# Routing four graphs at a time, and a second bank for the values product, in a graph-attention and mixture-of-experts kernel

## The chip, the cores and the metric

The kernel runs on one core of one Trainium2 chip. The metric is the device time of one execution in microseconds (us). The engines are called by their short names: PE (matrix products), DVE (vector), ACT (scalar, activations), POOL (GpSimd) and SP (the queue that issues most transfers).

## The reference, cut to what matters

```python
# x: 64 graphs x 128 nodes x 512, adj: 64 x 128 x 128, 16 heads of 32
h = layernorm(x)
a = q(h) @ k(h).T * 512**-0.5 + (adj + adj)      # per head, 128 x 128
a = softmax(where(any(a != 0), a, -inf))
x = x + (a @ v(h)) @ Wo.T
h = layernorm(x)                                  # 8192 tokens
s = maximum(h @ gate_W + gate_b, 1e-4)            # 8 experts
p = softmax(s); top 2 experts of each token
w = maximum(p, 0.1); w = w / (sum of w over the two)
out = x + sum over the two of w * (h @ expert_W[e] + expert_b[e]) / 2
```

## The kernel before, in words

The program has two phases. Phase A does the attention of the 64 graphs and the routing of their tokens; phase B does the experts' products over the token lists that phase A wrote to memory (`x_lists`). The change touches phase A alone.

**Turns and quarters.** Every engine's program in phase A is one loop, `for t in range(-6, 72)` over turns and `for c in range(4)` over the quarters of a turn. In turn t the scores and exponentials belong to graph t, the transposes of the probabilities to graph t-1, the products with values (`times_v`, into bank `ps_o`) and the copy `oT` to graph t-2, the output projection, residual and second norm to graphs t-3 and t-2. The projections go by pairs of graphs, one unit of 24 matmuls in each quarter (`big`): in an even turn Q, Q, V, V, in an odd turn O, K, O, K. Two banks `ps_p` take them in alternation: a unit waits until the unit two quarters earlier has been read (`wait_bank`). In the first and third quarter of the odd turn stand the two O units; quarter 1 and 3 of an even turn also transpose the normalised rows (`transposes`, "X", into `ps_m`). A unit of K or Q is read by ACT (high part) and then by DVE (`low_part`, the low part), one quarter after it was made, and on DVE behind that quarter's `attention_max`.

**The two halves of V.** A V unit makes 256 columns in a `ps_p` bank and then 264 columns (256 values and 8 gate columns), called `G_V`, in `ps_g`. Both V units of a pair use the same `G_V`, so the second half of V unit 1 waits for `v_done` of V unit 0, that is for ACT's three copies of it (L654 to L659). ACT makes them in the next quarter, behind the exponentials of the quarter before, and those wait for DVE's `amax`.

**Routing.** DVE routes the tokens of a pair p of graphs in five functions of small instructions (128 x 16 elements, mostly), each of which waits for the one before it: `gate_scores(p)` in quarter 2 and `choose(p)` in quarter 3 of the odd turn 2p+5, then `weigh(p)` and `find_places(p)` together in quarter 1 of the even turn 2p+6, all of them last in their quarter. Between them ACT takes one exponential (`eexp`), and PE counts the tokens per expert in quarter 1 of turn 2p+6 with three small matmuls into `G_P`, 24 columns of `ps_g` (L595 to L597), once `choose` has written `mask_sum`. V unit 0 of that turn waits, ahead of its second half, for the first step of `find_places`, because `G_P` shares a bank with `G_V`. `find_places` adds the running fill of each expert's list and writes the rows `pos`. POOL then issues the scatters, `scatter(p, a)`: two indirect DMAs a graph from `xn2`, one graph in each turn, in turn b+6 for graph b. `xn2` has 4 buffers, `pos` has 2, `gate_x` has 8.

**Ahead of the loop's steady part**, PE turns Wo, multiplies it with the gate's weights (`wo_times_gate`, with the columns `O_W` and `O_S` in `ps_o`), and `times_v` of graph 0 waits until these are read. **At the end of phase A**, from turn 62 on, DVE also splits the experts' weights (`expert_lo`, L974), in the order of `LO_AT`, and then makes the table of tiles for phase B (L1046 to L1069) and the last two splits.

Of the kernel before, what the change touches and what calls it, by code (L numbers as in the profile page):

```python
# [17 lines left out]
P = 128  # L18
B = 64
D = 512  # L20
DC = D // P
# [3 lines left out]
E = 8  # L25
# [23 lines left out]
C_ALL = C_DUM + E  # L49

# [72 lines left out]
def phase_a(nc, v):  # L123
# [9 lines left out]
    with mem:  # L133
# [23 lines left out]
        gate_x = sb("gate_x", [P, 8, E])  # L157
        gate_x1 = sb("gate_x1", [P, 4, E])
        all_one = sb("all_one", [P, P])
# [12 lines left out]
        xn2 = sb("xn2", [P, 4, W])  # L172
# [5 lines left out]
        score, dlt, eexp, eq, key, score2, em = (sb(n, [P, 2, E]) for n in ("score", "dlt", "eexp", "eq", "key", "score2", "em"))  # L178
        mask = sb("mask", [P, K, 2, E])
        mask_sum = sb("mask_sum", [P, 3, E], bf16)  # L180
        m1, m2, kmax, den, e2 = (sb(n, [P, 2]) for n in ("m1", "m2", "kmax", "den", "e2"))
        wgt = sb("wgt", [P, K, 2])
        wtot = sb("wtot", [P, 2])
        place = sb("place", [P, 2, E])
        place_k = sb("place_k", [P, K, 2, E])
        posf = sb("posf", [P, K, 2])
        pos = sb("pos", [P, 2, K, 2], i32)
        comb_k = sb("comb_k", [P, K, 2, E])
# [10 lines left out]
        G_V, G_P = ps_g[:, 0:D // 2 + E], ps_g[:, 3 * P:3 * P + 3 * E]  # L199
        G_O = ps_m[:, 0:D // 2 + E]  # L200
        O_W, O_S = ps_o[:, 0:DC * E], ps_o[:, DC * E:DC * E + E]
# [28 lines left out]
        scattered = sems("scattered", 4)  # L230
# [220 lines left out]
        def _(pe):  # L451
# [23 lines left out]
            def project(t, c):  # L475
# [16 lines left out]
                elif kind == "V":  # L492
# [6 lines left out]
                    if 2 * n + part:  # L499
                        pe.wait_ge(v_done, 2 * n + part)  # L500
                    if part == 0 and okp((t - 6) // 2):
                        pe.wait_ge(place_step, PLACE * ((t - 6) // 2) + 1)
                    for i in range(DC):
                        last = three(G_V, xT_hi[:, r, i, own], xT_lo[:, r, i, own], w_hi["v"][:, i, WIDE], w_lo["v"][:, i, WIDE], i == 0, i == DC - 1)
# [28 lines left out]
            def transpose_probs(b, c):  # L533
                n = DC * b + c
                pe.wait_ge(prob_done, n + 1)
                if n >= 1:
                    pe.wait_ge(pT_done, n)
                for h in range(HC):
                    last = nc.tensor.transpose(ps_t[:, P * h:P * h + P], prob[:, b % 2, c, h, :], ident)  # L539
                last.then_inc(pT_full, 1)  # L540

            def times_v(b, c):
                n = DC * b + c
                pe.wait_ge(pT_done, n + 1)
                if c == 0:
                    pe.wait_ge(v_done, b + 1)
                    if b >= 1:
                        pe.wait_ge(oT_done, b)
                    else:
                        pe.wait_ge(w_lo_done["o"], SPLITS["o"] + 1)  # L550
                        pe.wait_ge(gate_sum_done, 1)
# [25 lines left out]

            pe.wait_ge(ident_in, 16)

            for t in range(FIRST, LAST + 1):  # L580
                for c in range(DC):
# [8 lines left out]
                    p = (t - 6) // 2  # L590
                    if c == 1 and t % 2 == 0 and okp(p):
                        pe.wait_ge(route_step, ROUTE * p + 16)
                        if p >= 1:
                            pe.wait_ge(place_step, PLACE * (p - 1) + 1)
                        mm(G_P, tri[:, :], mask_sum[:, :, :].rearrange("p a e -> p (a e)"), start=True, stop=False)  # L595
                        mm(G_P[:, E:3 * E], ones[:, :], mask_sum[:, 0:2, :].rearrange("p a e -> p (a e)"), start=False, stop=False)
                        mm(G_P[:, 2 * E:3 * E], ones[:, :], mask_sum[:, 0, :], start=False, stop=True).then_inc(place_full, 1)  # L597
# [8 lines left out]
        def _(act):  # L606
# [24 lines left out]
            def read_projection(t, c):  # L631
# [17 lines left out]
                else:  # L649
# [5 lines left out]
                    nc.scalar.activation(vv[:, b % 4, RIGHT], G_V[:, LEFT], ACT.Copy)  # L655

                    if b >= 8:
                        act.wait_ge(x1_done, b - 7)
                    nc.scalar.activation(gate_x[:, b % 8, :], G_V[:, D // 2:D // 2 + E], ACT.Copy, scale=sdev1[:, b % 8:b % 8 + 1]).then_inc(v_done, 1)  # L659
# [27 lines left out]
            def second_norm(b):  # L687
                k = b % 4
                act.wait_ge(rstd2_step, RSTD * b + RSTD)
                if b >= 4:  # L690
                    act.wait_ge(scattered[b % 4], 32 * (b // 4))
                nc.scalar.activation(xn2[:, k, 0:D], xres[:, b % 2, :], ACT.Identity, bias=off2[:, k:k + 1], scale=rstd2[:, k:k + 1]).then_inc(xn2_done, 1)

            for t in range(FIRST, LAST + 1):
                for c in range(DC):
# [32 lines left out]
                    p = (t - 5) // 2  # L728
                    if c == 3 and t % 2 and okp(p):
                        act.wait_ge(route_step, ROUTE * p + 5)  # L730
                        nc.scalar.activation(eexp[:, :, :], dlt[:, :, :], ACT.Exp).then_inc(gexp_done, 1)
# [33 lines left out]
        def _(dve):  # L765
# [87 lines left out]
            def residual(b):  # L853
# [5 lines left out]
                tt(gate_x1[:, k, :], G_O[:, D // 2:D // 2 + E], gate_x[:, b % 8, :], ALU.add).then_inc(x1_done, 1)  # L859
# [5 lines left out]
            wide = lambda w: w[:, :].unsqueeze(2).to_broadcast([P, 2, E])  # L865
            rev = const[:, C_REV:C_REV + 2 * E].rearrange("p (a e) -> p a e", a=2)

            def gate_scores(p):

                step = [0]  # L870

                def link(ins):
                    step[0] += 1
                    ins.then_inc(route_step, 1)
                    dve.wait_ge(route_step, ROUTE * p + step[0])


                dve.wait_ge(rstd2_step, RSTD * (2 * p + 1) + RSTD)
                if p == 0:
                    dve.wait_ge(gate_sum_done, 1)  # L880
                    dve.wait_ge(small_in, 16)
                k = 2 * (p % 2)
                for r in range(2):
# [3 lines left out]
                for r in range(2):  # L887
# [3 lines left out]
                link(ts(score[:, :, :], score[:, :, :], GATE_EPS, None, ALU.max))  # L891
                link(nc.vector.tensor_reduce(m1[:, :], score[:, :, :], axis=AX.X, op=ALU.max))
                link(tt(dlt[:, :, :], score[:, :, :], wide(m1), ALU.subtract))

            def choose(p):

                step = [5]

                def link(ins):
                    step[0] += 1  # L900
                    ins.then_inc(route_step, 1)
                    dve.wait_ge(route_step, ROUTE * p + step[0])

                link(tt(eq[:, :, :], score[:, :, :], wide(m1), ALU.is_equal))
                link(tt(key[:, :, :], eq[:, :, :], rev, ALU.mult))
                link(nc.vector.tensor_reduce(kmax[:, :], key[:, :, :], axis=AX.X, op=ALU.max))
                link(tt(mask[:, 0], key[:, :, :], wide(kmax), ALU.is_equal))
                link(nc.vector.scalar_tensor_tensor(out=score2[:, :, :], in0=mask[:, 0], scalar=-BIG, in1=score[:, :, :], op0=ALU.mult, op1=ALU.add))
                link(nc.vector.tensor_reduce(m2[:, :], score2[:, :, :], axis=AX.X, op=ALU.max))
                link(tt(eq[:, :, :], score2[:, :, :], wide(m2), ALU.is_equal))  # L910
                link(tt(key[:, :, :], eq[:, :, :], rev, ALU.mult))
                link(nc.vector.tensor_reduce(kmax[:, :], key[:, :, :], axis=AX.X, op=ALU.max))
                link(tt(mask[:, 1], key[:, :, :], wide(kmax), ALU.is_equal))
                if p >= 1:
                    dve.wait_ge(place_full, p)
                link(tt(mask_sum[:, 0:2, :], mask[:, 0], mask[:, 1], ALU.add))

            def weigh(p):

                step = [16]  # L920

                def link(ins):
                    step[0] += 1
                    ins.then_inc(route_step, 1)
                    dve.wait_ge(route_step, ROUTE * p + step[0])

                dve.wait_ge(gexp_done, p + 1)
                nc.vector.tensor_reduce(den[:, :], eexp[:, :, :], axis=AX.X, op=ALU.add)
                link(tt(em[:, :, :], eexp[:, :, :], mask[:, 1], ALU.mult))
                nc.vector.reciprocal(wgt[:, 0, :], den[:, :])  # L930
                link(nc.vector.tensor_reduce(e2[:, :], em[:, :, :], axis=AX.X, op=ALU.max))
                link(tt(wgt[:, 1, :], e2[:, :], wgt[:, 0, :], ALU.mult))
                link(ts(wgt[:, :, :], wgt[:, :, :], W_THRES, None, ALU.max))
                link(tt(wtot[:, :], wgt[:, 0, :], wgt[:, 1, :], ALU.add))
                link(nc.vector.reciprocal(wtot[:, :], wtot[:, :]))
                link(nc.vector.scalar_tensor_tensor(out=wgt[:, :, :], in0=wgt[:, :, :], scalar=1.0 / K, in1=wtot[:, :].unsqueeze(1).to_broadcast([P, K, 2]),
                                                    op0=ALU.mult, op1=ALU.mult))
# [452 lines left out]
```

## Time and profile before

| | |
|---|---|
| median of 3 runs | 1661.66 us (1660.23 to 1663.96) |
| the profiled execution: its own time, its span | 1662.81 us, 1661.0 us |
| PE busy | 1550.8 us (93%) |
| DVE, POOL, ACT busy | 1215.8, 974.0, 955.9 us |
| granted TensorE clock, mean | 0.970 |
| phase A | to about 1194 us of the span; phase B from there to the end |

The span is the time from the first to the last instruction of one profiled execution; the execution's own time is 1.8 us longer. Busy times say how much of the span an engine had work in flight. PE's matmuls are pipelined, so a busy PE can still lose time between two starts; the distance from one start to the next in the timeline shows it.

### The profile page before, as it was taken

The numbers are of one execution on the slowest core, as the hardware profiler recorded it, in microseconds if no ns is written. First come the engines' busy times: TensorE is split into PE (matmuls) and PEld (weight loads), VectorE is DVE, ScalarE is ACT, GpSimd is POOL, SyncE is SP. The second block draws the span as 40 slices with busy tenths as digits, with TensorE's granted clock in tenths as the row PEclk, the third lists the DMA queues.
The fourth block names the chain that finished last, engine by engine and source line by source line (L and its number), as shares of the span: only waits on it lengthen the run. The fifth ranks groups of instructions, "written<-read, shape, count | busy, mean of one in ns | idle before, by whom it ended". The sixth has DMA issues, their size and how long they took to land. (4 is left out here: it accounts for less than half of the span.)

```text
span 1661.0 us, 45460 instructions
## 1 busy us (share of the span) xinstructions
PE 1550.8 (93%) x12808; PEld 1410.9 (85%) x12808; DVE 1215.8 (73%) x4952; ACT 955.9 (58%) x3129; POOL 974.0 (59%) x1788
## 2 busy tenths in 40 slices
PE   6999999999999999999999999966189999999996
PEld 6999999999999999999999999955167777777775
DVE  5578888888888888888888788877745555555554
ACT  4687777777777777777777777775111111111111
POOL 3255666566666666566665666556235565565655
PEclk9999999999999999999999999977599999999998
DMA  6787988789888888888887888794658898898886
GB/s 226 194 233 199 257 241 241 237 248 253 246 241 240 244 247 239 237 239 247 228 244 225 246 233 228 221 293 142 217 102 158 168 174 164 162 169 165 164 160 106
DMA packets 188629, 351.98 MB, mean 212 GB/s; under 512 B 20960, under 2 KB 30304, under 8 KB 188256
## 3 DMA queue, kind: packets, MB, share of 16 engines
q1 hardware_dynamic: 135520, 238.47, 51.7%
q0 software_dynamic: 29680, 69.55, 21.6%
q10 hardware_dynamic: 23184, 41.05, 8.0%
q8 instruction: 109, 1.79, 0.5%
q14 instruction: 136, 1.11, 0.2%
HBM read 189.48 MB, written 159.52 MB: 210 GB/s over the span
## 5 line engine op out<-in xcount | busy, mean ns | idle before, releaser
L678 ACT ACTIVATE prob<-prob,nmax 128x128 f32<-128x128 f32 x1024 | 398.8, 395 | 175.3 <-DVE amax L833 168.8
L1146 POOL TENSOR_TENSOR prob<-prob,rinv 128x512 f32<-128x512 f32 x256 | 261.4, 1042 | 241.3 <-DVE rinv L850 241.2
L829 DVE CUSTOM_DVE_ANT_0 prob<-ps_s,bias 128x128 f32<-128x128 f32 x1024 | 237.7, 287 | 142.1 <-PE ps_s L530 106.5
L1343 POOL DMA_INDIRECT out<-yt,token x135 | 211.6, 1567 | 196.3 <-DMA out<-yt,token 72.3
L1281 ACT ACTIVATE xgT_hi<-ps_x 128x512 fp32r<-128x512 f32 x135 | 80.7, 598 | 386.8 <-PE ps_x L1266 339.4
L1260 PE MATMUL ps_y<-we,xgT_hi 128*128 x540 | 260.8, 483 | 5.8 <-DVE xgT_lo L1300 5.8
L1261 PE MATMUL ps_y<-we,xgT_hi 128*128 x540 | 214.8, 398 | 0.0
L1262 PE MATMUL ps_y<-we,xgT_lo 128*128 x540 | 214.0, 396 | 0.0
L678 ACT ACTIVATION_READ_ACCUMULATOR prob<-prob,nmax 128x1 f32 x1024 | 196.7, 192 | 0.0
L833 DVE TENSOR_REDUCE amax<-prob 128x4 f32<-128x512 f32 x256 | 175.6, 686 | 8.9
L539 PE MATMUL ps_t<-const,prob 128*128 128x128 f32 x1024 | 164.8, 284 | 15.2 <-ACT pT L716 12.1
L1300 DVE TENSOR_TENSOR xgT_lo<-ps_x,xgT_hi 128x512 fp32r<-128x512 f32 x135 | 93.2, 690 | 105.6 <-ACT xgT_hi L1281 102.4
L1266 PE MATMUL ps_x<-const,xg 128*128 128x128 f32 x540 | 147.5, 276 | 21.1 <-DMA xg<-x_lists 21.1
L1156 POOL DMA_INDIRECT x_lists<-xn,pos x128 | 133.6, 1044 | 43.5 <-issue 37.7
L716 ACT ACTIVATE pT<-ps_t 128x512 f32<-128x512 f32 x256 | 152.1, 594 | 11.9 <-PE ps_t L539 9.7
L455 PE MATMUL ps_p<-xT_hi,wk_hi 128*128 128x256 f32 x512 | 150.9, 295 | 1.8 <-DVE xT_lo L815 1.8
L530 PE MATMUL ps_s<-ks,qs 96*128 96x128 f32 x1024 | 145.8, 265 | 7.2 <-issue 4.9
L1260 PEld LDWEIGHTS ps_y<-we,xgT_hi 128*128 128x128 f32 x540 | 102.7, 190 | 56.3 <-issue 9.3
L455 PE MATMUL ps_p<-xT_hi,wq_hi 128*128 128x256 f32 x512 | 149.7, 292 | 0.6 <-DVE kT_lo L802 0.6
L456 PE MATMUL ps_p<-xT_lo,wk_hi 128*128 128x256 f32 x512 | 145.8, 285 | 0.0
L457 PE MATMUL ps_p<-xT_hi,wk_lo 128*128 128x256 f32 x512 | 145.7, 285 | 0.0
L530 PEld LDWEIGHTS ps_s<-ks,qs 96*128 96x128 f32 x1024 | 138.7, 193 | 7.9 <-issue 7.7
(191 smaller groups left out, 4770.4 us busy)
## 6 DMA issues: line engine op xcount, KB each, us to landing
ks<-kq_parts SPq DMA_DIRECT2D x192, 256.0 KB, 4.2
qs<-kq_parts SPq DMA_DIRECT2D x192, 256.0 KB, 6.3
xg<-x_lists ACTq DMA_DIRECT2D x135, 260.5 KB
xin<-x SPq DMA_DIRECT2D x64, 256.0 KB, 7.2
kq_parts<-kT_hi SPq DMA_DIRECT2D x32, 512.0 KB, 3.8
kq_parts<-kT_lo SPq DMA_DIRECT2D x32, 512.0 KB, 4.8
kq_parts<-qT_hi SPq DMA_DIRECT2D x32, 512.0 KB
kq_parts<-qT_lo SPq DMA_DIRECT2D x32, 512.0 KB
```

The costliest lines, as they stand in the source:

```text
L455: mm(out_, lhs_hi, rhs_hi, start=first, stop=False)
L530: last = mm(ps_s[c % 2][:, P * h:P * h + P], qs[:, r, h, c, :], ks[:, r, h, c, :], start=True, stop=True)
L539: last = nc.tensor.transpose(ps_t[:, P * h:P * h + P], prob[:, b % 2, c, h, :], ident)
L678: last = nc.scalar.activation(prob[:, r, c, h, :], prob[:, r, c, h, :], ACT.Exp, bias=nmax[:, r, i:i + 1], scale=-1.0, accum_out=rsum[:, r ...
L716: nc.scalar.activation(pT[:, c].rearrange("p h t -> p (h t)"), ps_t[:, :], ACT.Copy).then_inc(pT_done, 1)
L829: last = nc.vector.tensor_tensor_reduce(out=prob[:, r, c, h, :], in0=ps_s[c % 2][:, P * h:P * h + P], in1=bias[:, b % 4, :], scale=-1.0, s ...
L833: nc.vector.tensor_reduce(amax[:, r, HC * c:HC * c + HC], prob[:, r, c, :, :], axis=AX.X, op=ALU.max, apply_absolute_value=True).then_inc( ...
L1146: tt(prob[:, r, q], prob[:, r, q], rinv[:, r, HC * q:HC * q + HC].unsqueeze(2).to_broadcast([P, HC, P]), ALU.mult)\
L1260: nc.tensor.matmul(ps_y[r][:, :], xgT_hi[:, r, c, :], hi, start=c == 0, stop=False)
L1261: nc.tensor.matmul(ps_y[r][:, :], xgT_hi[:, r, c, :], lo, start=False, stop=False)
L1262: last = nc.tensor.matmul(ps_y[r][:, :], xgT_lo[:, r, c, :], hi, start=False, stop=c == DC - 1)
L1343: pool.indirect_dma_start(out=out, out_offset=bass.IndirectOffsetOnAxis(ap=token[:, m, :], axis=0), in_=yt[:, r, :], in_offset=None, compu ...
```

## The change

Routing goes by groups (`GROUPS`): 14 groups of four graphs and then 4 groups of two. The parts of a group's routing stand in other quarters, spread over three turns. With `last` the group's last graph: `gate_scores` in quarter 3 of turn last+3, `choose` in quarter 0 of turn last+4, ACT's exponential in quarter 1, `weigh` (without its last three steps) and PE's counting in quarter 2 of that turn, and the rest of `weigh` (now `combine`) with `find_places` in quarter 0 of turn last+5. The counting takes 8 matmuls for four graphs, 4 for two. A scatter still takes one graph a turn, in turn b+8 for graphs in groups of four and b+6 in groups of two, so that turns 62 and 63 have two each. `xn2` has 8 buffers, `pos` 3, `gate_x` 6.

The second half of V unit 0 goes into `ps_o`, the bank of the products with values, and only V unit 1 uses `ps_g`. V unit 0 waits for `oT_done` of the graph two turns back, and `times_v` of an odd turn waits for ACT's copies of V unit 0. The wait for `find_places` stands at V unit 1. `O_W` and `O_S` move to `ps_t`, so the first transposes of probabilities wait for their readers.

```diff
+GROUPS = [(4 * q, 4) for q in range((B - 8) // 4)] + [(b, 2) for b in range(B - 8, B, 2)]
+LAST_OF = {b + n - 1: g for g, (b, n) in enumerate(GROUPS)}
...
-        G_V, G_P = ps_g[:, 0:D // 2 + E], ps_g[:, 3 * P:3 * P + 3 * E]
+        G_V, G_P = [ps_o[:, 0:D // 2 + E], ps_g[:, 0:D // 2 + E]], ps_g[:, 3 * P:3 * P + 5 * E]
...
-                    if 2 * n + part:
-                        pe.wait_ge(v_done, 2 * n + part)
-                    if part == 0 and okp((t - 6) // 2):
-                        pe.wait_ge(place_step, PLACE * ((t - 6) // 2) + 1)
+                    if part == 0 and ok(t - 2):
+                        pe.wait_ge(oT_done, t - 1)
+                    if part == 1 and n >= 1:
+                        pe.wait_ge(v_done, 2 * n)
+                    if part == 1 and t - 5 in LAST_OF:
+                        pe.wait_ge(place_step, PLACE * LAST_OF[t - 5] + 1)
...
+                    if b % 2 and ok(b + 3):
+                        pe.wait_ge(v_done, b + 4)
...
+            def places(g):
+                first, n = GROUPS[g]
+                pe.wait_ge(route_step, ROUTE * g + 16)
+                pe.wait_ge(v_done, min(B, first + n + 6))
+                if g >= 1:
+                    pe.wait_ge(place_step, PLACE * (g - 1) + 1)
+                rows = lambda w, a, b: w[:, E * a:E * b]
+                sums = mask_sum[:, :, :].rearrange("p a e -> p (a e)")
+                mm(rows(G_P, 0, n + 1), tri[:, :], rows(sums, 0, n + 1), start=True, stop=False)
+                for i in range(1, n):
+                    mm(rows(G_P, i + 1, n + 1), ones[:, :], rows(sums, 1, n + 1 - i), start=False, stop=False)
+                for i in range(n):
+                    last = mm(rows(G_P, 0, 1), ones[:, :], rows(sums, i + 1, i + 2), start=False, stop=i == n - 1)
...
-                    if not odd and okp(p):
-                        if c == 1:
-                            weigh(p)
-                            find_places(p)
...
-                        if c == 2:
-                            gate_scores(p)
-                        if c == 3:
-                            choose(p)
+                    if c == 3 and t - 3 in LAST_OF:
+                        gate_scores(LAST_OF[t - 3])
+                    if c == 0 and t - 4 in LAST_OF:
+                        choose(LAST_OF[t - 4])
+                    if c == 2 and t - 4 in LAST_OF:
+                        weigh(LAST_OF[t - 4])
+                    if c == 0 and t - 5 in LAST_OF:
+                        combine(LAST_OF[t - 5])
+                        find_places(LAST_OF[t - 5])
```

The bodies of the five DVE functions keep their instructions, with n graphs of 8 experts in place of two; `combine` first waits for the scatters of the graphs eight back (`scattered`), as `weigh` did for four back.

## Rows read from the trace of the kernel before

**Rows 1.** Busy time by stretch: start and end, length, each engine, clock, DMA share.

```profile
93.95:126.97 33.02, 33.02 (x331) 32.48 (x330) 22.69 (x104) 27.19 (x92) 17.71 (x39) 1.00 0.78 210
499.68:533.78 34.10, 33.92 (x333) 32.82 (x332) 28.61 (x141) 26.53 (x93) 21.90 (x43) 1.00 0.89 252
143.06:1067.17 924.11, 916.44 (x8940) 885.88 (x8939) 773.70 (x3781) 716.02 (x2515) 588.98 (x1152) 1.00 0.84 240
```

**Rows 2.** Waits of the whole span: who waited for whom, us, times, longest.

```profile
PEld ps_p L455 <- DVE qT_lo L804: 12.1, 28, 0.8
...
PEld ps_g L455 <- ACT gate_x L659: 6.4, 28, 0.2
```

**Rows 3.** Timeline of PE, V unit 1 in a turn with routing: start, length.

```profile
534.64 0.60 PE L472 MATMUL ps_m<-const,xin 128*128 128x128 f32 x4
535.41 0.39 PE L455 MATMUL ps_p<-wv_hi,xT_hi 128*128 128x256 f32 x1 [0.17 <-DVE qT_lo L804]
...
536.82 0.28 PE L457 MATMUL ps_p<-wv_hi,xT_lo 128*128 128x256 f32 x1
537.12 0.39 PE L455 MATMUL ps_g<-wv_hi,xT_hi 128*128 128x264 f32 x1
```

**Rows 4.** Timeline of PE, V unit 1 before the routing has begun.

```profile
125.39 0.28 PE L457 MATMUL ps_p<-wv_hi,xT_lo 128*128 128x256 f32 x1
125.51 0.28 PE L455 MATMUL ps_g<-wv_hi,xT_hi 128*128 128x264 f32 x1
```

**Rows 5.** DVE's busy time, quarters of turns 3 and 4: stretch, length, busy.

```profile
93.95:98.83 4.88, 1.90 (x11) 1.00 1.05 234
...
102.57:106.31 3.74, 2.86 (x15) 1.00 0.20 71
...
110.05:114.91 4.86, 2.86 (x15) 1.00 1.06 235
114.91:119.07 4.16, 2.88 (x12) 1.00 1.05 369
...
122.80:126.97 4.17, 3.41 (x14) 1.00 0.94 295
```

**Rows 6.** Timeline of DVE, the routing of one pair, first and last instructions.

```profile
516.50 0.36 DVE L884 SCALAR_TENSOR_TENSOR score<-gate_sum,shift,gate_x 128x8 f32<-128x8 f32 x2
...
521.47 0.14 DVE L904 TENSOR_TENSOR eq<-score,m 128x16 f32<-128x16 f32 x1
...
529.40 0.15 DVE L928 TENSOR_REDUCE den<-eexp 128x2 f32<-128x16 f32 x1
...
531.15 0.16 DVE L936 SCALAR_TENSOR_TENSOR wgt<-wgt,wtot 128x4 f32<-128x4 f32 x1
531.35 0.19 DVE L938 TENSOR_TENSOR comb_k<-mask,wgt 128x32 f32<-128x32 f32 x1
...
532.66 0.17 DVE L968 CAST pos<-posf 128x4 int32<-128x4 f32 x1
```

**Rows 7.** Timeline of PE, first and last of the three counting matmuls.

```profile
526.86 0.18 PE L595 MATMUL ps_g<-mask_sum,tri 128*128 128x24 bf16 x1
...
526.91 0.17 PE L597 MATMUL ps_g<-mask_sum,ones 128*128 128x8 bf16 x1
```

**Rows 8.** Timelines of ACT and PE: the copy of V unit 0, the next `times_v`.

```profile
502.72 0.25 ACT L659 ACTIVATE gate_x<-ps_g,sdev 128x8 f32<-128x8 f32 x1
...
505.10 1.08 PE L553 MATMUL ps_o<-pT,vv 128*32 128x128 f32 x32
```

**Rows 9.** Timeline of DVE at the end of phase A.

```profile
1159.69 0.14 DVE L904 TENSOR_TENSOR eq<-score,m 128x16 f32<-128x16 f32 x1
...
1161.96 2.50 DVE L974 TENSOR_TENSOR we<-we 128x512 fp32r<-128x512 f32 x4
1164.38 0.16 DVE L928 TENSOR_REDUCE den<-eexp 128x2 f32<-128x16 f32 x1
...
1179.11 0.16 DVE L1032 CAST ends<-fill 1x8 int32<-1x8 f32 x1
```

More of the change, by code:

```diff
@@ L177, in phase_a @@
         var2, nwt2, rstd2, nmu2, off2, shift2 = (sb(n, [P, 4]) for n in ("var2", "nwt2", "rstd2", "nmu2", "off2", "shift2"))
[L178 to L188, printed above, removed]
+        score, dlt, eexp, eq, key, score2 = (sb(n, [P, 4, E]) for n in ("score", "dlt", "eexp", "eq", "key", "score2"))
+        em = score2
+        mask = sb("mask", [P, K, 4, E])
+        mask_sum = sb("mask_sum", [P, 5, E], bf16)
+        m1, m2, kmax, den, e2 = (sb(n, [P, 4]) for n in ("m1", "m2", "kmax", "den", "e2"))
+        wgt = sb("wgt", [P, K, 4])
+        wtot = sb("wtot", [P, 4])
+        place = sb("place", [P, 4, E])
+        place_k = sb("place_k", [P, K, 4, E])
+        posf = sb("posf", [P, K, 4])
+        pos = sb("pos", [P, 3, K, 4], i32)
+        comb_k = sb("comb_k", [P, K, 4, E])
         spare_end = sb("spare_end", [P, E - 1, 1 + E])
@@ L589, in _ @@
                     transposes(t, c)
[L590 to L597, printed above, removed]
+                    if c == 2 and t - 4 in LAST_OF:
+                        places(LAST_OF[t - 4])
                     if (t, c) == (-1, 2):
@@ L654, in read_projection @@
                     nc.scalar.activation(vv[:, b % 4, LEFT], bank[:, LEFT], ACT.Copy)
[L655 to L659, printed above, removed]
+                    nc.scalar.activation(vv[:, b % 4, RIGHT], G_V[part][:, LEFT], ACT.Copy)
+                    if b >= 6:
+                        act.wait_ge(x1_done, b - 5)
+                    nc.scalar.activation(gate_x[:, b % 6, :], G_V[part][:, D // 2:D // 2 + E], ACT.Copy, scale=sdev1[:, b % 8:b % 8 + 1]).then_inc(v_done, 1)
             def read_transposes(t, c):
@@ L727, in _ @@
                         first_norm(t + 3 + c)
[L728 to L731, printed above, removed]
+                    if c == 1 and t - 4 in LAST_OF:
+                        g = LAST_OF[t - 4]
+                        n = GROUPS[g][1]
+                        act.wait_ge(route_step, ROUTE * g + 5)
+                        nc.scalar.activation(eexp[:, 0:n, :], dlt[:, 0:n, :], ACT.Exp).then_inc(gexp_done, 1)
                     if t == -4 and c == 1:
@@ L863, in residual, with chain, gate_scores @@
                 nc.vector.bn_aggr(mv2[:, k, :], st2[:, k, :]).then_inc(mean2, 1)
[L865 to L870, printed above, removed]
+            rev = lambda n: const[:, C_REV:C_REV + E].unsqueeze(1).to_broadcast([P, n, E])
+            wide = lambda w, n: w[:, 0:n].unsqueeze(2).to_broadcast([P, n, E])
+            def chain(base, done, signal):
+                step = [base + done]
                 def link(ins):
                     step[0] += 1
[L874 to L879, printed above, removed]
+                    ins.then_inc(signal, 1)
+                    dve.wait_ge(signal, step[0])
+                return link
+            def gate_scores(g):
+                first, n = GROUPS[g]
+                link = chain(ROUTE * g, 0, route_step)
+                dve.wait_ge(rstd2_step, RSTD * (first + n - 1) + RSTD)
+                if g == 0:
                     dve.wait_ge(gate_sum_done, 1)
                     dve.wait_ge(small_in, 16)
-                k = 2 * (p % 2)
-                for r in range(2):
+                k = first % 4
+                for r in range(n):
                     last = nc.vector.scalar_tensor_tensor(out=score[:, r, :], in0=gate_sum[:, :], scalar=shift2[:, k + r:k + r + 1],
@@ new lines, in landed, with combine @@
+            def landed(graphs):
+                for b in graphs:
+                    dve.wait_ge(scattered[b % 8], 32 * (b // 8 + 1))
+            def combine(g):
+                first, n = GROUPS[g]
+                link = chain(ROUTE * g, 22, route_step)
+                link(nc.vector.scalar_tensor_tensor(out=wgt[:, :, 0:n], in0=wgt[:, :, 0:n], scalar=1.0 / K,
+                                                    in1=wtot[:, 0:n].unsqueeze(1).to_broadcast([P, K, n]), op0=ALU.mult, op1=ALU.mult))
+                link(tt(comb_k[:, :, 0:n, :], mask[:, :, 0:n, :], wgt[:, :, 0:n].unsqueeze(3).to_broadcast([P, K, n, E]), ALU.mult))
+                landed(range(max(0, first - 8), first - 8 + n))
+                k = first % 8
+                tt(xn2[:, k:k + n, D + 1:W], comb_k[:, 0, 0:n], comb_k[:, 1, 0:n], ALU.add)
+                link(nc.vector.tensor_copy(xn2[:, k:k + n, D], const[:, C_TOK + first:C_TOK + first + n]))
@@ new lines, in find_places @@
+            def find_places(g):
+                _, n = GROUPS[g]
+                link = chain(PLACE * g, 0, place_step)
+                r = g % 3
+                old, new = fill[:, g % 2, :], fill[:, 1 - g % 2, :]
+                places = G_P.rearrange("p (a e) -> p a e", a=5)
+                dve.wait_ge(place_full, g + 1)
+                tt(place[:, 0:n, :], places[:, 1:n + 1, :], old.unsqueeze(1).to_broadcast([P, n, E]), ALU.add)
+                link(tt(new, places[:, 0, :], old, ALU.add))
@@ L970, in expert_lo @@
+                if g >= 3:
+                    before, m = GROUPS[g - 3]
+                    landed(range(before, before + m))
+                link(nc.vector.tensor_copy(pos[:, r, :, 0:n], posf[:, :, 0:n]))
             def expert_lo(e):
@@ L1188, in _ @@
                         tt(bias[:, k, :], bias[:, k, :], bias[:, k, :], ALU.add).then_inc(bias_done, 1)
-                    a = t % 2
-                    p = (t - 6 - a) // 2
-                    if c == (3 - 2 * a if t < B else 3) and okp(p):
-                        scatter(p, a)
+                    if c == (3 if t >= B or not odd else 1):
+                        for b in range(B):
+                            g, a = GROUP_OF[b]
+                            if t == GROUPS[g][0] + GROUPS[g][1] + 4 + a:
+                                scatter(b)
                     p = (t + 6) // 2
```

153 lines of the change are left out of this document (61 added, 92 removed).

## The prediction

> **What bounds the kernel now.** I read the page first: PE is in flight for 93% of the span, and no other engine for more than 73%. Such a number says which engine to look at, not whether it loses time. So I cut phase A into stretches and compared two of the same content. A pair of graphs is two turns, and in the steady part every pair asks PE for the same units. From 93.95 to 126.97 us (turns 3 and 4), when every unit of a steady pair is there but the routing has not begun, a pair takes 33.02 us; a pair in the middle of phase A takes 34.10; and the 27 pairs from turn 6 to turn 59 take 924.11, or 34.23 each [rows 1]. The rest of the row tells who differs: PE is busy throughout in both, ACT does about the same (27.2 and 26.5 us), and DVE goes from 22.7 to 28.6 us. The routing is the difference. It puts next to nothing on PE itself, so 1.2 us per pair are lost on PE to waiting for somebody else.
>
> The list of waits names them: 28 times a V unit waits for `qT_lo` of DVE, and 28 times its second half waits for ACT's copy of the other V unit [rows 2]; 28 is the number of even turns, 6 to 60, that have both routing and V. The durations in that list understate the loss, since a wait that begins while the last matmul is still in flight counts from its end. The timeline shows it better. In V unit 1 the transposes of X start at 534.64 and take four steps, about 0.44 us, and the unit could follow at about 535.08; it starts at 535.41. Its second half starts 0.30 us behind the matmul ahead of it [rows 3], where the distance within a unit is 0.12. In a pair ahead of the routing the same place shows 0.12 [rows 4], although both V units use one `ps_g` bank there too. So the shared bank costs nothing while ACT is on time. ACT is late because its exponentials wait for DVE's `amax`, and DVE is late because it stands in a routing chain. All of these waits go back to one cause.
>
> **How late DVE may be.** This decides what the new placing is worth, so I make a small account of it. The calm pair leaves DVE, per quarter, in the odd turn 2.98 us in quarter 0 and about 0.88 in each of the other three (the row of quarter 2 stands for them), and in the even turn 2.00, 1.28, about 0.8 and 0.76 [rows 5]. A routing piece longer than the free time leaves DVE behind by the difference, and the next free times work it off. Before, `gate_scores` takes 1.43 us (seven instructions of 0.17 to 0.22 with the waits between them), `choose` 2.27 [rows 9], and `weigh` with `find_places` 3.43, from 529.40 to 532.83 [rows 6]. The account runs: 1.43 in odd quarter 2 leaves 0.55; 2.27 in odd quarter 3 leaves 1.94; even quarter 0 clears it; 3.43 in even quarter 1 leaves 2.15, then about 1.4 and 0.6. PE is seen to wait after 2.15 and not after 1.94, so the tolerance lies near 2 us, at least where a long quarter follows.
>
> **The change part by part.**
>
> *DVE.* Four graphs in one chain cost little more than two: an instruction over 32 elements a partition takes 0.19 us against 0.17 over 16 [rows 6]. With four more small instructions in `gate_scores` (0.18 each) I get for four graphs: gate 2.15, choose 2.5, weigh's first eight steps 1.8 (1.75 from 529.40 to 531.15), combine and find_places 1.9. That is 8.35 us in place of two times 7.1. The new account: gate in even quarter 3 leaves 1.4; choose in odd quarter 0, where 2.98 are free, leaves 0.9; quarter 1 clears it; weigh in quarter 2 leaves 0.9; quarter 3 leaves none; combine and find_places in even quarter 0 fit into its 2.00. The peak of 1.4 lies under the tolerance, and the second pair of each four has no routing at all. So I forecast that the loss goes: 924.11 - 27 x 33.02 = 32.6 us, and 1.2 for turn 60, which I price as one pair more: **33.8 us**. Against it I set 1.0 us for short new waits; the bounds are 0 and 0.4 us (one gap as that of V unit 1 in [rows 3]) in each of 14 groups, 5.6.
>
> *PE's counting.* It is really on PE's path. Three matmuls start 0.025 us apart [rows 7]. The quarter with them lasts 4.33 us (525.56 to 529.89, from scores to scores), the same quarter without them 4.16 [rows 5]; this 0.17 is already in the 33.8. Eight for four graphs cost 0.17 + 5 x 0.025 = 0.30 if the rest is a cost of switching, and 0.45 if it goes by number; 14 groups give 4.2 to 6.3, and I take **4.5**, near the first, since it is the spacing that the rows show. The last four groups' counting falls after PE has run out of units. The Trainium skill, "TensorE: Matmul & The Clock Gate", section "LDWEIGHTS (loading the stationary operand)", has a load of 128 columns last 107 ns; it would make these eight 0.86 us a group and the whole term 12 us, 7.5 worse. The trace does not agree: these bf16 loads follow each other at 0.025, and the page's own section on fast weight loads makes an exception for such weights.
>
> *The banks.* V unit 0 into `ps_o` must wait for `oT_done`, set in quarter 0, two quarters earlier: nothing. V unit 1 then needs nothing of unit 0. By [rows 4] this is worth nothing once DVE is on time, and where DVE is late it takes away the 0.18 us of the second half. I count it in the 33.8 and not again. The new wait is that of `times_v` in the odd turn for ACT's copy of unit 0. ACT's copy ended at 502.97 and the product began at 505.10 [rows 8], 2.1 us to spare with ACT late. Behind that wait stand all of PE's queue and ACT's read of V unit 1. Price: nothing. The wait for `find_places` moves to V unit 1, three quarters behind the chain: nothing; before, it bound V unit 0 by some 0.1 us.
>
> *Scatters, rings, start.* POOL issues one graph's scatter in a turn as before, in the same quarters, two turns later; the rings of 8 and 3 give the two turns back, and the DMA queues carry the same bytes. Nothing, covered by POOL's idle 40%. In turns 62 and 63 a second scatter puts some 2.6 us on POOL, most of it into idle time; 0.5 us. The first transposes of probabilities now wait for `gate_sum`, which DVE makes about when PE arrives: 0 to 0.5, taken as nothing.
>
> *The end.* From 1157.9 to about 1193 DVE works without a gap: residual, choose, expert split, weigh and find_places, and so on. Here its work counts in full. After the last residual before, choose (1159.69 to 1161.96) and weigh of graphs 60 and 61 follow [rows 9]; in the new order both stand ahead of it, choose in quarter 0 and weigh in quarter 2 of turn 65, partly in a gap of 2.8 us where DVE waits for PE. Left out of the last stretch are 2.27 and weigh's 1.3, 3.6 us; routing would end at about 1175.5 instead of 1179.1 of the old scale. Bounds 0 (choose only delays the residual instead) and 4. Taken: **3.3**.
>
> *Sum.* 33.8 - 1.0 - 4.5 - 0.5 + 3.3 = 31.1 us. From the profiled execution's 1662.8 that gives 1631.7; it was 1.15 above the median of the runs, so about **1631**.
>
> **The rivals.**
>
> 1. *The gain is halved.* A turn with routing may cost what it cost before, because DVE's chain for four graphs runs over two neighbouring quarters, even 3 and odd 0 (4.65 us against 3.74 free), and ACT drags on behind it. Then only the number of such turns falls, from 28 to 14: 33.8/2 = 16.9, with counting as in the old turns and 3.3 of the end, 20 us: 1643. For it: the tolerance of 2 us was seen in other quarters, and O units wait for the residual too. Against: the peak is 1.4.
>
> 2. *33.02 is not the floor.* Turns 3 and 4 have no scatters, and DMA share goes from 0.78 to 0.89 [rows 1]. If a fifth to a third of the 1.2 us is due to them and stays, 7 to 11 us are not won: 1638 to 1642. Against: the waits on PE name DVE and ACT, and none names a DMA.
>
> 3. *Slower: PE waits for V unit 0's copy.* In 29 odd turns `times_v` could wait for ACT. It begins to cost when ACT is 2.1 us later than in [rows 8]; it decides when it costs over 31.1/29 = 1.07 us a pair, at 3.2 us later. At 3.5 later it takes 1.4 each, 41 us: 1672. ACT has about 6 us idle in a pair, and the change makes DVE's `amax` earlier, not later, in most turns; in the quarter in question the chain `gate_scores` stands behind the `amax` that the copy needs.
>
> 4. *No effect.* The waits would come back elsewhere at the same size, as when ACT sets the pace (its 27.2 of 33.02 us leave little): 1660 to 1663. But the calm pair has this same load of ACT.
>
> **How the numbers follow.** Forecast 0.70 (1625 to 1637 alone); rival 1 0.12, rival 2 0.09, rival 3 0.04, rival 4 0.05. The lower bound takes no new waits, counting at 4.2, and 2 us for the uncertainty of the end: 1626, and I go to 1624. The upper reaches to rivals 1 and 2: 1644. About 0.2% (3.3 us) is what a measurement can tell. Faster 0.91, same 0.04, slower 0.05.
>
> **What would show it.** In the changed profile: a pair without routing at 33.0 us and one with it at 33.3 to 33.5; the waits for `qT_lo` and `gate_x` gone from PE's list; DVE's busy time in phase A less by some 5.8 us per four graphs; four to eight counting matmuls 0.025 apart; the routing's end 3 to 4 us nearer to the last residual. It would be wrong if pairs with routing take 34 or more (rival 1), if all pairs take 33.3 or more (rival 2), or if `times_v` has a wait for ACT's `gate_x` (rival 3). Phase B should not change.

## The result: slower, and the profile after

The changed kernel took **1680.74 us** (median of 4 runs, 1676.13 to 1683.84) against 1662.47 for the kernel before beside it (1660.23 to 1663.96). The ratio is 1.0109, with a 95% interval of 1.0081 to 1.0136: slower by 1.1%, where 1631 us had been forecast. The profiled execution took 1676.13 us, with a span of 1674.3.

I cut it as [rows 1] cut the kernel before. The windows view of the changed kernel shows a pair without routing (193.82 on), a group of four graphs with its routing and the pair behind it (507.63 on), turns 6 to 59 (143.96 on), and two pieces of one quarter. The columns are those of [rows 1].

```profile
193.82:226.86 33.04, 33.04 (x331) 32.50 (x330) 23.27 (x105) 26.84 (x96) 22.28 (x44) 1.00 0.85 241
507.63:577.00 69.37, 66.81 (x667) 65.42 (x666) 56.40 (x249) 53.83 (x185) 43.70 (x87) 1.00 0.86 240
309.00:311.70 2.70, 1.04 (x17) 0.96 (x16) 2.47 (x13) 0.85 (x5) 1.08 (x2) 1.00 0.83 262
312.30:315.70 3.40, 3.40 (x18) 3.40 (x18) 3.15 (x18) 2.66 (x12) 1.71 (x8) 0.50 0.49 179
...
143.96:1079.29 935.33, 904.58 (x8970) 886.02 (x8969) 756.76 (x3352) 721.78 (x2491) 583.29 (x1148) 1.00 0.84 236
```

The calm pair is as forecast, 33.04 us, now with scatters in it. But a group of four takes 69.37 us where two calm pairs take 66.08, and turns 6 to 59 take 935.33, 11.2 more than [rows 1], where the sum had 27.1 less for these turns (32.6 - 1.0 - 4.5). The rest of the 13.3 us by which the span grew is small: 0.9 ahead of turn 6, 0.9 less from turn 60 to phase B, 2.0 more in phase B.

The list of PE's waits has the two that [rows 2] had, in another form: fewer and longer.

```profile
PE ps_p L462 <- DVE gate_x L881: 27.1, 18, 4.2
...
PE ps_p L462 <- DVE qT_lo L826: 12.5, 9, 1.8
```

PE waits for `gate_x`, that is for `residual`, ahead of the second O unit of the odd turn in which `choose` stands, and for `qT_lo` ahead of V unit 0 in the even turn with `combine` and `find_places`. In the group from 507.63 on the first is 1.28 us and makes a quarter of 5.45 us where 3.74 is usual (0.30 of it is the counting, as e4 shows below); the second is 1.27 and makes 5.29 of 3.73. These two quarters are the whole 3.3 us.

DVE is the late engine in both, so I read its timeline beside POOL's. The odd turn:

```profile
511.26 0.17 DVE L872 SCALAR_TENSOR_TENSOR rinv<-amax,rinv 128x8 f32<-128x8 f32 x1
511.34 0.18 DVE L925 TENSOR_TENSOR eq<-score,m 128x32 f32<-128x32 f32 x1
...
512.01 0.69 DVE L928 TENSOR_TENSOR mask<-key,kmax 128x32 f32<-128x32 f32 x1
512.74 0.96 DVE L929 SCALAR_TENSOR_TENSOR score<-mask,score 128x32 f32<-128x32 f32 x1
513.74 0.19 DVE L930 TENSOR_REDUCE m<-score 128x4 f32<-128x32 f32 x1
513.96 0.99 DVE L931 TENSOR_TENSOR eq<-score,m 128x32 f32<-128x32 f32 x1
514.99 0.33 DVE L932 TENSOR_TENSOR key<-eq,const 128x32 f32<-128x32 f32 x1
...
515.79 0.19 DVE L937 TENSOR_TENSOR mask_sum<-mask 128x32 bf16<-128x32 f32 x1
```

```profile
511.61 2.05 POOL L1160 TENSOR_TENSOR prob<-prob,rinv 128x512 f32<-128x512 f32 x2 [0.23 <-DVE rinv L872]
513.62 1.29 POOL L1197 TENSOR_TENSOR oT_lo<-oT,oT_hi 128x512 fp32r<-128x512 f32 x1
514.86 0.40 POOL L1202 TENSOR_TENSOR bias<-bias 128x128 f32<-128x128 f32 x1
```

Instructions of one size take 0.19 us or up to 1 us. The long ones end just after one of POOL's: 512.70 in the middle of the row of two `prob`, 513.70 behind the second `prob` (513.66), 514.95 behind `oT_lo` (514.91), 515.32 behind `bias` (515.26). The reduction between them takes its 0.19 while `oT_lo` runs. `choose` took 4.64 us in place of 2.5. The brackets of POOL's first row say why they meet: it waited for `rinv`, the instruction that stands right ahead of `choose`. In the even turn the same happens to `find_places`:

```profile
529.89 0.16 DVE L960 SCALAR_TENSOR_TENSOR wgt<-wgt,wtot 128x8 f32<-128x8 f32 x1
...
530.68 0.19 DVE L975 TENSOR_TENSOR place<-ps_g,fill 128x32 f32<-128x32 f32 x1
530.79 0.16 DVE L976 TENSOR_TENSOR fill<-ps_g,fill 128x8 f32<-128x8 f32 x1
530.98 1.95 DVE L978 TENSOR_TENSOR place_k<-place,mask 128x32 f32<-128x32 f32 x2
532.96 0.22 DVE L980 TENSOR_REDUCE posf<-place_k 128x8 f32<-128x64 f32 x1
533.22 0.95 DVE L984 CAST pos<-posf 128x8 int32<-128x8 f32 x1
```

`prob` ran from 530.84 to 532.88 and `oT_lo` from 532.84 to 534.14. `combine` and `find_places` took 4.3 us, not 1.9. This sets the theory for the runs, **collision**: POOL's long instructions hold up DVE's that read two inputs from SBUF. Its rival is **length**: a chain for four graphs is too long for one quarter, collision or not. Each run below was timed beside the kernel before on the same chip, and ratios are to that. The expectations say VectorE, GpSimd and TensorE for DVE, POOL and PE.

### The profile page after: what moved, and what is told of

It reads as the page before. It is cut to its first block and busy times, and to the rows that moved or that the text cites. A ratio compares the mean times of both kernels' runs of the same rounds, so it can differ in the third digit from the quotient of the medians.

```text
span 1674.3 us, 44992 instructions
## 1 busy us (share of the span) xinstructions
PE 1542.0 (92%) x12840; PEld 1414.1 (84%) x12840; DVE 1201.7 (72%) x4504; ACT 964.0 (58%) x3115; POOL 971.5 (58%) x1788
## 5 line engine op out<-in xcount | busy, mean ns | idle before, releaser
L1324 DVE TENSOR_TENSOR yt<-ps_y,e_bias 128x512 f32<-128x512 f32 x135 | 93.4, 692 | 75.5 <-DMA out<-yt,token 46.4
```

## The experiments

### Ahead of `inverse_sums` or behind it

`inverse_sums` is what releases POOL. In e1 both pieces stand ahead of it in the same quarter, in e2 only `choose`, in e3 only the other two; the comments name the runs.

```diff
+                    if c == 0 and t - 4 in LAST_OF:      # e1, e2
+                        choose(LAST_OF[t - 4])
+                    if c == 0 and t - 5 in LAST_OF:      # e1, e3
+                        combine(LAST_OF[t - 5])
+                        find_places(LAST_OF[t - 5])
                     if c == 0 and ok(t - 1):
                         inverse_sums(t - 1, 1)
```

> The changed kernel with choose, and combine with find_places, placed ahead of inverse_sums in the first quarter of their turns instead of behind it. Theory A (collision): VectorE's instructions with two SBUF inputs stand still while GpSimd runs prob, oT_lo and bias, which inverse_sums releases; ahead of it they run at 0.19 us, choose takes 2.5 us and not 4.7, combine with find_places 1.9 and not 4.3. TensorE's waits for gate_x (1.28 us) and qT_lo (1.27 us) in each of 14 groups fall under 0.3 us: 14 x 2.5 = 35 us less, 1641 to 1650 us; GpSimd's oT_lo then ends some 2.5 us later and may hold the O unit by up to 0.5 us (7 us in all). Theory B (length): the pieces for four graphs are too long for their quarters wherever they stand in them: 1680 us, waits as they were.

Measured: 1636.56 us, ratio 0.9837 (0.9818 to 0.9857). Moving both pieces ahead of two instructions took 44 us out of the changed kernel. It is 4 us below the range of theory A. Both waits are gone from turns 6 to 59 of PE's list. A group of four (the first row, counted from another quarter of the turn) takes 66.46 us by its windows view, two calm pairs and 0.4; turns 6 to 59 (the second row) take 898.54:

```profile
501.64:568.10 66.46, 66.46 (x666) 65.29 (x665) 52.10 (x249) 53.72 (x186) 43.65 (x86) 1.00 0.88 251
...
143.32:1041.86 898.54, 897.96 (x8970) 882.33 (x8969) 703.88 (x3355) 727.37 (x2494) 584.00 (x1148) 1.00 0.87 245
```

Length falls: the chain is as long as before in instructions, and it fits.

> The changed kernel with choose alone moved ahead of inverse_sums. Theory A: the wait for gate_x in the third quarter of the odd turn goes (14 x 1.3 = 18 us), the one for qT_lo stays: 1660 to 1665 us, somewhat less where TensorE's clock no longer falls behind the wait. Theory B: 1680 us.

Measured: 1648.60 us, ratio 0.9909 (0.9890 to 0.9928), 11 us below the range.

> The changed kernel with combine and find_places alone moved ahead of inverse_sums. Theory A: the wait for qT_lo in the even turn goes (14 x 1.27 = 18 us), the one for gate_x stays: 1660 to 1665 us. Theory B: 1680 us.

Measured: 1657.45 us, ratio 0.9960 (0.9946 to 0.9975), 3 us below the range. The waits that should stay stayed in e3: 1.28 to 1.6 us for `gate_x` in 13 groups. In e2 those for `qT_lo` shrank as well, to at most 0.9 us in 7 groups; `place_k` there took 0.67 us on average and not 0.84, so it met less of POOL's work. Where the two engines meet moves with PE's own delay. So the two gains, 32 and 23 us, add up to more than the 44 of both.

### POOL's instructions shortened, VectorE's program untouched

```diff
+                w = 4 if half and b in SMALL else P
-                    tt(prob[:, r, q], prob[:, r, q], ...)
+                    tt(prob[:, r, q, :, 0:w], prob[:, r, q, :, 0:w], ...)
```

and the same for `oT_lo` and `bias`, in the two turns of each group that matter (`SMALL` names their graphs).

> The changed kernel, its VectorE program untouched; in the two turns of each group where choose, combine and find_places run, GpSimd's prob (second half), oT_lo and bias cover 4 of 128 columns each. It leaves out most of that normalising, splitting and adding. Theory A: with GpSimd's instructions gone VectorE's are 0.19 us again at their old place, both waits go: 1638 to 1648 us. Theory B: 1680 us. A third theory, that VectorE's instructions are slow by their own form (4 graphs, broadcast inputs), gives 1680 us too, with mask at 0.69 us and place_k at 0.95 us as before.

Measured: 1634.29 us, ratio 0.9824 (0.9805 to 0.9843), 4 us below the range of theory A. DVE's instructions at their old place, behind `inverse_sums`, in its timeline:

```profile
496.84 0.19 DVE L928 TENSOR_TENSOR mask<-key,kmax 128x32 f32<-128x32 f32 x1
497.07 0.19 DVE L929 SCALAR_TENSOR_TENSOR score<-mask,score 128x32 f32<-128x32 f32 x1
...
497.51 0.19 DVE L931 TENSOR_TENSOR eq<-score,m 128x32 f32<-128x32 f32 x1
```

Neither their form nor their place makes them slow; POOL does. The time is less than e1's by no more than the intervals allow.

e4 also shows what the counting costs, since nothing else holds PE in its quarter. In all 14 groups the O unit behind the eight matmuls starts 1.06 us after the quarter's scores, and not 0.78, and the quarter takes 4.04 us, and not 3.74:

```profile
501.09 0.56 PE L539 MATMUL ps_s<-ks,qs 96*128 96x128 f32 x4
...
502.15 0.37 PE L462 MATMUL ps_p<-wo_hi,oT_hi 128*128 128x256 f32 x1
```

In e1 it starts later in 13 of the 14 groups, about 0.05 us behind the end of POOL's `oT_lo`, which the new order makes later. In one group, from POOL's and PE's timelines (its scores start at 501.64):

```profile
501.50 1.28 POOL L1197 TENSOR_TENSOR oT_lo<-oT,oT_hi 128x512 fp32r<-128x512 f32 x1
502.83 0.39 PE L462 MATMUL ps_p<-wo_hi,oT_hi 128*128 128x256 f32 x1
```

So the order of e1 has a small price of its own, 2.3 us in all.

### The operand moved out of SBUF

Here nothing is moved and POOL does all its work. `eq`, `key`, `score2`, `place`, `posf` and a copy of `score` live in spare columns of a PSUM bank.

```diff
+        at = lambda o: ps_g[:, o:o + 4 * E].rearrange("p (a e) -> p a e", a=4)
+        eq, place, score_p, key, score2 = at(264), at(296), at(336), at(424), at(456)
+        posf = ps_g[:, 328:328 + 4 * K].rearrange("p (k a) -> p k a", k=K)
...
+                dve.wait_ge(v_done, min(B, GROUPS[g][0] + n + 6))
+                nc.vector.tensor_copy(score_p[:, 0:n, :], score[:, 0:n, :])
...
-                        pe.wait_ge(place_step, PLACE * LAST_OF[t - 5] + 1)
+                        pe.wait_ge(place_step, PLACE * LAST_OF[t - 5] + PLACE)
```

The last edit makes V unit 1 wait for the last step of `find_places` and not for the first, because the later steps now read `ps_g` too.

> The changed kernel with every piece at its place behind inverse_sums, but eq, key, score2, place, posf and a copy of score in spare columns of the PSUM bank ps_g, so that each VectorE instruction of choose behind the first and of find_places has at most one input in SBUF (one more instruction, the copy). If it is two inputs in SBUF that GpSimd's instructions block: mask, score2, eq, key and place_k take 0.2 us each during prob and oT_lo, choose about 2.8 us, find_places about 1.4; both waits of TensorE go, 1636 to 1645 us. If GpSimd slows every VectorE instruction that touches SBUF, or if the length counts: 1675 to 1685 us.

Measured: 1647.89 us, ratio 0.9916 (0.9897 to 0.9935), 33 of the 44 us, and 3 us above the range. The timeline of DVE, with POOL's `prob` running from 502.83 to 504.87 and `oT_lo` from 504.83 to 506.12:

```profile
503.35 0.19 DVE L932 TENSOR_TENSOR mask<-ps_g,kmax 128x32 f32<-128x32 f32 x1
503.57 0.20 DVE L933 SCALAR_TENSOR_TENSOR ps_g<-mask,ps_g 128x32 f32<-128x32 f32 x1
503.80 0.19 DVE L934 TENSOR_REDUCE m<-ps_g 128x4 f32<-128x32 f32 x1
504.02 0.20 DVE L935 TENSOR_TENSOR ps_g<-ps_g,m 128x32 f32<-128x32 f32 x1
...
504.72 0.19 DVE L938 TENSOR_TENSOR mask<-ps_g,kmax 128x32 f32<-128x32 f32 x1
504.94 1.22 DVE L941 TENSOR_TENSOR mask_sum<-mask 128x32 bf16<-128x32 f32 x1
```

Nine instructions that ran under POOL's (502.89 to 504.91) took 0.2 us, and the one whose two inputs are both still in SBUF took 1.22 and ended at 506.16, just behind `oT_lo`. The instruction that I had left out of the edit is the control inside the run. It kept `choose` at 3.6 us, not the 2.8 expected, and PE waiting 0.25 to 0.57 us in 13 of the 14 groups; some 4 us of the profiled run's distance to e1 stood ahead of turn 6, apart from all this. For these forms the condition is two inputs in SBUF, not contact with SBUF. The Trainium skill, "SBUF — State Buffer", section "SBUF: two separate sides", says that GpSimd (POOL) and VectorE (DVE) share one pair of ports under an exclusive lock, taken by a VectorE instruction with two SBUF inputs or in a two-port performance mode, and that the loser stands still for the other's whole instruction; these rows agree. They do so for POOL's long instructions alone. In 11 groups of the changed kernel `dlt`, with two inputs in SBUF, met a small instruction of POOL with 2 elements a partition and was not lengthened:

```profile
508.57 0.73 POOL L1148 TENSOR_TENSOR rstd<-var,half 128x2 f32<-128x2 f32 x1 [0.18 <-POOL var L1147]
509.05 0.19 DVE L920 TENSOR_TENSOR dlt<-score,m 128x32 f32<-128x32 f32 x1
```

Why the small ones hold up nothing stays open.

### What fours, the bank and the places are worth

e6 is e1 with groups of two throughout (`GROUPS = [(b, 2) for b in range(0, B, 2)]`). e5 is e1 with both V units in `ps_g`, with the old waits:

```diff
-        G_V, G_P = [ps_o[:, 0:D // 2 + E], ps_g[:, 0:D // 2 + E]], ...
+        G_V, G_P = [ps_g[:, 0:D // 2 + E], ps_g[:, 0:D // 2 + E]], ...
```

e11 has both edits: of the change the places are left, with the deeper buffers and `O_W` and `O_S` in `ps_t`. e7 is the kernel before with the second bank alone, that is with the changed kernel's `G_V`, its `O_W` and `O_S` in `ps_t`, and the waits that go with them.

> The kernel of e1 with routing in groups of two throughout: the five places in the schedule are kept, but every pair goes through them. If the places were what counts and not the four graphs: choose 2.3 us and combine with find_places 1.7 us fit into the first quarters, TensorE waits nowhere, and the counting costs 28 x 0.2 us, 1634 to 1640 us. If VectorE needs the unrouted pair to recover: a wait of 0.5 to 1 us in each pair comes back, 1650 us or more.

> The kernel of e1 (choose, combine and find_places ahead of inverse_sums) without the part of the change on banks: both V units again put their second half into ps_g. If a late VectorE was the cause of the waits on ps_g, VectorE being on time leaves the bank nothing to win: 1635 to 1639 us, as e1's 1636.6. If the second bank gives 0.2 us or more in each of 30 pairs by itself: 1643 us or more.

> The kernel of e6 (pairs, pieces ahead of inverse_sums) with both V units in ps_g: of the whole change only the new places are left, and the order inside two of them. If they are all of the gain: 1632 to 1638 us. If fours or the bank carry a part: 1640 us or more.

> The kernel before with the part of the change on banks alone: V unit 0's second half goes into ps_o. Its routing stays in pairs at the old places, so VectorE and with it ScalarE are as late as before. The gap of 0.18 us ahead of the second halves goes in each of 28 pairs, and the start of V unit 1 still waits for qT_lo: 1655 to 1660 us. If the bank is worth nothing by itself: 1662 us. If the new wait of the products with values for ScalarE's copy bites: over 1664 us.

Measured: e6 1634.47 us, 0.9825 (0.9793 to 0.9857); e5 1635.31, 0.9831 (0.9796 to 0.9866); e11 **1631.87, 0.9821 (0.9801 to 0.9842)**; e7 1656.81, 0.9953 (0.9936 to 0.9970). Each lies in the range of one of its theories, e11 at the edge. The ratios of e1, e5, e6 and e11 all lie within one another's intervals. In e11 the windows view gives a pair with its routing and 28.30 us of DVE work, as much as in [rows 1], at PE's own pace:

```profile
297.00:330.20 33.20, 33.20 (x334) 32.65 (x334) 28.30 (x140) 26.85 (x94) 22.00 (x44) 1.00 0.88 250
```

So routing four graphs at once gave no time that could be measured, and the second bank none once DVE is on time. The bank is worth 7 us where DVE is late: in e7 V unit 0's quarter is 3.73 us again (mostly 3.9 to 4.3 before), and V unit 1 waits 0.33 us or more for `qT_lo`.

> The changed kernel, its pieces behind inverse_sums, with routing in groups of two: the kernel of e6 but for the order. A VectorE instruction that meets GpSimd waits for it whatever its own size, so choose and combine with find_places end as late as for four graphs, and now in each of 28 pairs: with 2.5 us of waits in each, 1634 + 70 = 1704 us, 1690 at least if the second wait of a pair is partly covered by the first. If the length of the chain for four graphs is what the changed kernel suffers from, groups of two are faster than it: under 1670 us.

e10 is e6 with the pieces behind, where the changed kernel had them. Measured: 1682.98 us, ratio 1.0124 (1.0096 to 1.0152), 48 us over e6. `choose` for two graphs took 4.5 to 5.1 us there, in nearly every pair, as long as for four. Shorter chains did not help, which speaks against length once more. The time is 7 us less than the least I expected: `gate_x` is late by 1.0 to 1.6 us in nearly every pair (40.2 us in PE's list), but V unit 0's quarter is mostly 4.0 us and not 5.3.

### Another quarter, and the last turns

```diff
-                    if c == 0 and t - 4 in LAST_OF:
-                        choose(LAST_OF[t - 4])
...
                     low_part_of_x(t, c)
+                    if c == 1 and t - 4 in LAST_OF:
+                        choose(LAST_OF[t - 4])
                     if odd and c == 1 and ok(t - 3):
                         residual(t - 3)
```

> The kernel of e1 with choose one quarter later, in the odd turn's second quarter ahead of residual, where GpSimd runs none of the long instructions but VectorE has only 0.88 us free of its own work. If VectorE may be 2 us late anywhere, as the prediction took from the even turn: 2.5 - 0.9 = 1.6 us late, no wait, 1637 us. If the tolerance in the odd turn is nearer to 0.4 us (choose was 4.7 - 3.0 = 1.7 us late there in the changed kernel and TensorE waited 1.28): a wait for gate_x of 1.2 to 2 us in 14 groups, 1654 to 1665 us.

Measured: 1655.09 us, ratio 0.9950 (0.9934 to 0.9967). The profiled execution is the fastest of the six, 1647.43. There is next to no collision (0.1 us of `bias`) and still a loss: the quarter of the second O unit takes 5.06 us or more in every group, and not 4.04 as in e4. That unit waits for `residual`, which stands right behind `choose`:

```profile
508.59 0.15 DVE L881 TENSOR_TENSOR gate_x<-ps_m,gate_x 128x8 f32<-128x8 f32 x1
508.89 0.36 PE L462 MATMUL ps_p<-wo_hi,oT_hi 128*128 128x256 f32 x1 [0.59 <-DVE gate_x L881]
```

`gate_x` ends 2.55 us later than in a pair without routing, the whole length of `choose` and not 1.6: the free time of the quarter does not lie ahead of `residual`. PE loses 1.0 us, so `residual` may be 1.5 us late at no cost.

e8 goes back to the order behind `inverse_sums` from turn 60 on.

> The kernel of e1, but from turn 60 on the pieces stand behind inverse_sums as in the changed kernel: there TensorE has few units left and waits for GpSimd's prob (6 waits, 10.2 us in e1, against 3 and 5.0 us in the changed kernel). If the later inverse_sums is what holds the last turns: 1.5 us less than e1, 1635 us. If the collision costs as much there as the earlier inverse_sums gives back: 1636.6 us, as e1.

Measured: 1640.12 us, ratio 0.9857 (0.9829 to 0.9885). This was no gain; whether it is a loss against e1 the intervals leave open.

## Why the prediction was wrong

**The step that failed** is the duration of the routing's instructions at their new places, "gate 2.15, choose 2.5, weigh's first eight steps 1.8, combine and find_places 1.9". Where no long instruction of POOL runs beside them it is right: in e1 `choose` took 2.44 us and `combine` with `find_places` 1.83. At the places of the changed kernel they meet POOL's `prob` and `oT_lo` and took 4.64 and, in most groups, 4.3. With that, "the peak of 1.4 lies under the tolerance" falls. In the account's own terms the odd quarter 0 ends with 1.4 + 4.64 - 2.98 = 3.06 us of lateness and not 0.9. The trace agrees: DVE takes up quarter 1's scores 3.69 us after PE has started them at 512.51, where a pair without routing has 0.74, so it is 2.95 late.

```profile
516.20 0.29 DVE L851 CUSTOM_DVE_ANT_0 prob<-ps_s,bias 128x128 f32<-128x128 f32 x1 [0.21 <-DVE mask_sum L937]
```

In the even turn of that group DVE is still 1.07 us late when `combine` comes, where the account had none, and 1.07 + 4.28 - 2.00 = 3.35 behind it; the timeline has 3.34.

The kernel before shows the effect in its grouping by line, among neighbours of the same size at 0.14 to 0.21 us, and in the very pair of [rows 6], right behind the first row of `weigh`. I passed over both. There `em` ends at 530.06, just behind POOL's `oT_lo` at 530.02:

```profile
L929 DVE TENSOR_TENSOR em<-eexp,mask 128x16 f32<-128x16 f32 x32 | 18.7, 583 | 0.0
...
528.72 1.30 POOL L1183 TENSOR_TENSOR oT_lo<-oT,oT_hi 128x512 fp32r<-128x512 f32 x1
529.48 0.58 DVE L929 TENSOR_TENSOR em<-eexp,mask 128x16 f32<-128x16 f32 x1
```

So about 0.4 of the 1.75 us from which `weigh` was scaled was collision; it took 1.37 in most groups of e1, where 1.8 had been forecast. How much of the old kernel's lateness this collision makes, no run tests.

**The tolerance** of about 2 us was somewhat large, and not the error. What may be late is the instruction that releases PE. `gate_x` of `residual` came 2.95 us late in the changed kernel, 2.55 in e12 and 1.91 in e9, against a pair without routing, and PE's O unit 1.43, 1.03 and 0.39 later than in e4: 1.5 us are free each time. For V unit 0 in the even turn it was 3.34 late and 1.51 lost, 1.8 free. The free time of 0.88 that the account gave the odd quarter 1 was wrong: back to back, that quarter's work takes DVE 3.47 of 3.74 us (516.20 to 519.67). Without the collision, in e1, `residual` is about 0.7 us late.

**The other steps** can be tested in e1, which is the change without the collision. For turns 6 to 59 the loss that goes, less counting and new waits, was put at 32.6 - 4.5 - 1.0 = 27.1 us; they went from 924.11 to 898.54, 25.6. The counting was right: 0.30 us a group in e4, 4.2 in all, for a forecast of 4.5, with four matmuls at 0.20 in e6. That fits the 0.17 of three and 0.025 for each further one, and not the 0.86 us for eight, the estimate by the page of the Trainium skill that the prediction names. The new waits were mis-sized, 2.3 us for 1.0, and they are for POOL's `oT_lo`, which no term had. DVE's busy time in turns 6 to 59 went from 773.70 to 703.88, 5.2 us per four graphs where 5.8 had been worked out. From turn 60 to phase B it took 129.9 us before and 126.65 in e1, 3.25 less, where 1.2 for turn 60, 3.3 for the end and -0.5 for the scatters make 4.0. In the runs e1 gains 26.2 of the 31.1 us.

**The rivals.** None of the four was what happened. The first came nearest, since it has routed turns as slow as before, but through length. The third, the only slower one, had `times_v` wait for ACT's copy of V unit 0; no such wait is in the list. That 33.02 is the floor, which the second rival doubted, was right: 33.04 in the changed kernel, with scatters. The chance of 0.05 for slower left out the one mechanism that could reach it: what POOL does at the time and place to which an instruction is moved.

## What to carry to other kernels

Before moving VectorE's (DVE's) instructions, look at what GpSimd (POOL) runs at the new place, and above all whether the instruction ahead of it is the one that releases GpSimd; here the order against two instructions was worth 44 us, and routing four graphs at once nothing that could be measured. If one line of instructions is several times as long as its neighbours of the same size, compare its end with GpSimd's ends before taking a duration for a forecast. If a two-input instruction cannot move, one operand in PSUM kept it free here. And count lateness at the instruction that releases the waiting engine: free time that lies behind it is of no help.

## What the runs showed that I had not expected

**Which instructions stand still.** In the changed kernel, beside the two-input ones, POOL's long instructions held up `pos`, a cast with one input (0.17 us alone, 0.95 met), which in e9 with its input in PSUM took 0.17. Reductions (0.19), `residual`'s sums with one input in PSUM (0.41) and `bn_stats` (0.69) took the same with and without POOL. POOL's own `prob` was not slowed: a piece took 1.03 to 1.05 us in nearly all cases, in the changed kernel as in e1.

**The clock behind a stall.** In two of the 14 groups a wait of 1.6 us was followed by a fall of PE's granted clock from full to half (2.4 to 1.2 GHz), for 3.4 us in the windows above; that quarter took 7.36 us and not 5.8, with matmuls about 0.21 us apart and not 0.12:

```profile
309.80 0.24 PE L602 MATMUL ps_g<-mask_sum,ones 128*128 128x8 bf16 x4
311.70 0.36 PE L462 MATMUL ps_p<-wo_hi,oT_hi 128*128 128x256 f32 x1 [1.66 <-DVE gate_x L881]
```

The waits of 1.28 us did not do this, and neither did one of 1.59 us nor one of 1.78 for `qT_lo` in an even turn, so the length of the wait alone does not decide it. What does stays open.
